# Self-attention scores in four PSUM banks, GpSimd's weighing behind VectorE's, and an early load of the second expert's W1

## The reference, cut to what matters

```
scores = where(causal, q @ k.T / sqrt(32), -1e30)
attn   = softmax(scores)
mask   = clip((256 + z - dist) / 256, 0, 1)      # z: one span per batch and head
attn   = attn * mask
attn   = attn / (attn.sum(-1) + 1e-8)
out    = attn @ v
```

## Time and profile before

| what | value |
|---|---|
| median of 3 runs | 3295.51 us (3294.92 to 3296.34) |
| the profiled execution | 3303.09 us |
| its span | 3301.3 us |
| TensorE busy, whole span | 2990.0 us (91%) |
| VectorE, ScalarE, GpSimd busy | 1859.6, 1063.0, 943.3 us |
| self-attention, about | 343 to 1830 us of the span |
| dispatch | 2577 to 2681 us |
| experts | 2681 to 3165 us |
| mean granted TensorE clock | 0.943 |

### The profile page before, as it was taken

The page is one execution under the profiler, slowest core; times in us unless marked ns, Lnnn a source line. Parts: engine busy times, 40 slices in busy tenths (PEclk is TensorE's granted clock), DMA queues, the critical chain, the costliest instruction groups (busy, mean ns, idle before and its releaser), DMA issues. The chain is left out here.

```text
span 3301.3 us, 54795 instructions
## 1 busy us (share of the span) xinstructions
PE 2990.0 (91%) x19242; PEld 1673.0 (51%) x19242; DVE 1859.6 (56%) x2220; ACT 1063.0 (32%) x2510; POOL 943.3 (29%) x606
## 2 busy tenths in 40 slices
PE   8998799999999999999999789999999787777778
PEld 6876333333333333333333678888888343333335
DVE  4355878787887878787883345555554510000038
ACT  3222344444444444444444223333333100101123
POOL 0000554445444444445454022222222000000013
PEclk9999899999999999999999889999999888878889
DMA  4453512121212212131200411111111669999954
GB/s 166 178 204 128 128 49 62 51 70 44 70 53 55 69 48 60 52 73 43 69 16 4 150 42 64 64 64 64 64 64 65 243 249 420 420 421 420 421 226 162
DMA packets 181219, 438.54 MB, mean 133 GB/s; under 512 B 17470, under 2 KB 51928, under 8 KB 156457
## 3 DMA queue, kind: packets, MB, share of 16 engines
q1 hardware_dynamic: 174057, 425.19, 36.8%
q10 hardware_dynamic: 6976, 10.75, 0.9%
HBM read 351.74 MB, written 83.89 MB: 132 GB/s over the span
## 5 line engine op out<-in xcount | busy, mean ns | idle before, releaser
L785 ACT ACTIVATE B_e<-B_pS 128x512 f32<-128x512 f32 (+3 forms) x1280 | 619.2, 534 | 850.0 <-PE B_pS L865 427.9
L640 POOL TENSOR_TENSOR B_em<-B_e,B_mask 128x1024 f32<-128x1024 f32 (+1 forms) x320 | 670.9, 2098 | 730.7 <-ACT B_e L785 693.9
L703 DVE TENSOR_REDUCE mx<-B_pM 128x4 f32<-128x2048 f32 (+2 forms) x299 | 588.9, 1969 | 38.7 <-PE B_pM L847 20.3
L865 PE MATMUL B_pS<-B_qs,B_ks 128*128 128x512 f32 (+3 forms) x1280 | 505.2, 447 | 43.4 <-issue 19.7
L696 DVE SCALAR_TENSOR_TENSOR B_em<-B_mask,B_e 128x1024 f32<-128x1024 f32 (+1 forms) x320 | 354.4, 1108 | 257.9 <-PE B_pN L895 256.3
L865 PEld LDWEIGHTS B_pS<-B_qs,B_ks 128*128 128x128 f32 x1280 | 227.8, 192 | 363.1 <-issue 238.5
L883 PE MATMUL B_pD<-B_e,B_tiny 128*32 128x512 f32 (+3 forms) x2560 | 310.0, 557 | 0.0
L889 PE MATMUL B_pD<-B_em,B_ones 128*32 128x512 f32 (+3 forms) x2560 | 301.2, 543 | 0.3 <-DVE B_em L696 0.3
L895 PE MATMUL B_pN<-B_em,B_v 128*32 128x512 f32 (+3 forms) x2560 | 293.4, 530 | 0.0
L2089 PE MATMUL E_pI<-ring,hT 128*32 128x512 f32 x1024 | 184.5, 815 | 101.1 <-DMA ring<-in_L_ffn_e_W_dram 57.8
L2012 DVE TENSOR_TENSOR E_ug<-E_pT,bT 128x32 f32 x32 | 5.7, 192 | 445.2 <-PE E_pT L2099 445.2
(11 more groups left out here) (288 smaller groups left out, 4764.2 us busy)
## 6 DMA issues: line engine op xcount, KB each, us to landing
ring<-in_L_ffn_e_W_dram SPq DMA_DIRECT2D x128, 1024.0 KB, 21.8
ring<-in_L_ffn_e_Wg_dram SPq DMA_DIRECT2D x64, 1024.0 KB, 23.6
B_qs<-q_hi SPq DMA_DIRECT2D x64, 256.0 KB, 4.5
B_ks<-k_hi SPq DMA_DIRECT2D x64, 256.0 KB, 3.9
E_xq<-xT_sc ACTq DMA_DIRECT2D x18, 512.0 KB, 10.3
ring<-x_sc SPq DMA_DIRECT2D x36, 256.0 KB, 2.6
qc<-in_x_dram SPq DMA_DIRECT2D x34, 256.0 KB, 2.7
qc<-a_sc SPq DMA_DIRECT2D x34, 256.0 KB, 3.0
```

What stands on the lines that cost most here:

```text
L640: nc.gpsimd.tensor_tensor(em[:, f % SLOTS_EM, DVE_HEADS:, w0:], e[:, f % SLOTS_E, DVE_HEADS:, w0:], mask[:, DVE_HEADS:, u0:u0 + BLK - w0], ...
L703: nc.vector.tensor_reduce(mx[:, :, qt, c], pM[:, :, 0:w], AX.X, ALU.max).then_inc(max_taken, 1)
L785: nc.scalar.activation(e[:, f % SLOTS_E, h, w0:], pS[:, h % SBANKS, w0:], ACT.Exp, scale=SCALE).then_inc(exp_ready, 1)
L865: last = nc.tensor.matmul(pS[:, h % SBANKS, w0:], ks[:, kb // NT, h, kb % NT * P:(kb % NT + 1) * P], qs[:, qb, h, w0:], start=True, stop=( ...
```

## The change

Self-attention:
- TensorE makes all four heads' scores of a step at once, into four banks: `B_pS` keeps two (heads 0 and 3), and heads 1 and 2 go to banks 2 and 3 of `B_pM`, which the units also use. So head 1's product waits until the last unit's maxima have been taken from banks 2 and 3 (`half_taken`), and a unit waits for the exponentials of heads 0 to 2 of its group's step (`exps_ahead`). The unit moves into the mix, between the products with 1e-8 and those with ones.
- VectorE reduces banks 2 and 3 first and then banks 0 and 1, two instructions for one. The reduction moves ahead of the weighing and of block 0's ramps; the other ramps stay at the end of the group, now right behind the weighing and the reciprocals. The reciprocals come in four parts over four groups.
- GpSimd's weighing of a step waits for VectorE's of the same step (`masked`).
- ScalarE's copies of the denominators and numerators after a block change places.

Experts:
- Six pieces of expert 0 are loaded at the start of dispatch and one behind each chunk's load. W1 of expert 1 goes to the upper half of `qc` during the end of dispatch (three pieces after the last chunk, the fourth after the output product) under a semaphore of its own; the ring's W1 pieces are then refilled with expert 2's while expert 1 runs. The first two experts are written out ahead of TensorE's loop.

```diff
-SBANKS = 2
+SBANKS = 4
+PARTS = 4
...
-        pS = ps("B_pS", [P, SBANKS, BLK], F32)
+        pS = ps("B_pS", [P, 2, BLK], F32)
+        score_bank = [pS[:, 0, :], pM[:, 2, :], pM[:, 3, :], pS[:, 1, :]]
...
-            events += [(min(ENDS[qb] + 5, STEPS + 1), "out", qb) for qb in range(BPB)]
+            events += [(min(ENDS[qb] + 3 + PARTS, STEPS + 1), "out", qb) for qb in range(BPB)]
...
                 pool.wait_ge(exp_ready, it * HPG * STEPS + HPG * (f + 1) + SBANKS)
                 pool.wait_ge(mixed, it * STEPS + STEPS + f + 1 - SLOTS_EM)
+                pool.wait_ge(masked, it * STEPS + f + 1)
                 nc.gpsimd.tensor_tensor(em[:, f % SLOTS_EM, DVE_HEADS:, w0:], e[:, f % SLOTS_E, DVE_HEADS:, w0:],
                                         mask[:, DVE_HEADS:, u0:u0 + BLK - w0], ALU.mult).then_inc(masked_last, 1)

             def divide(it, qb):
                 n = it * BPB + qb
-                pool.wait_ge(inverse, n * 2 + 2)
+                pool.wait_ge(inverse, (n + 1) * PARTS)
                 pool.wait_ge(num_out, n + 2)
                 pool.wait_ge(stored, 16 * n)
...
                         weigh(it, f)
-                    if f - 5 in ENDS:
-                        divide(it, block_end(f - 5))
+                    if f - 3 - PARTS in ENDS:
+                        divide(it, block_end(f - 3 - PARTS))
                 divide(it, BPB - 1)
...
                 w = BLK if c < qb else (qt + 1) * P
                 dve.wait_ge(max_ready, it * STEPS + n + 1)
-                nc.vector.tensor_reduce(mx[:, :, qt, c], pM[:, :, 0:w], AX.X, ALU.max).then_inc(max_taken, 1)
+                nc.vector.tensor_reduce(mx[:, 2:HPG, qt, c], pM[:, 2:HPG, 0:w], AX.X, ALU.max).then_inc(half_taken, 1)
+                nc.vector.tensor_reduce(mx[:, 0:2, qt, c], pM[:, 0:2, 0:w], AX.X, ALU.max).then_inc(max_taken, 1)
                 if n in ENDS:
+                    dve.wait_ge(half_taken, it * STEPS + n + 1)
                     dve.wait_ge(max_taken, it * STEPS + n + 1)
                     nc.vector.tensor_reduce(mm[:, :].rearrange("p (h q) -> p h q", h=HPG), mx[:, :, :, 0:qb + 1],
...
                 at_least(dve, mrow_loaded, 16 * r)
                 nc.vector.tensor_copy(mrow[:, :], pM[0:ROWS, 0, 0:P]).then_inc(mrow_ready, 1)
-            def invert(it, qb, half):
+            def invert(it, qb, part):
                 dve.wait_ge(den_out, it * BPB + qb + 2)
-                at = slice(half * BLK // 2, (half + 1) * BLK // 2)
+                at = slice(part * BLK // PARTS, (part + 1) * BLK // PARTS)
                 nc.vector.reciprocal(sums[:, 1, at], sums[:, 1, at]).then_inc(inverse, 1)
             RAMPS = 0
             dve.sem_inc(max_taken, EARLY)
+            dve.sem_inc(half_taken, EARLY)
             dve.sem_inc(neg_ready, EARLY_ROWS)
             take_turned(0)
             dve.wait_ge(spans_loaded, 16)
...
                         take_spans(it, (it + 1) * HPG, it + 2)
+                    n, later = unit_of(f)
+                    if n == 0 or (n - 1 in ENDS and not (final and later)):
+                        take_turned(rows_before(it + later, n))
+                    if not (final and later):
+                        reduce_unit(it + later, n)
                     if f == STEPS and not final:
                         dve.wait_ge(masked_last, it * STEPS + STEPS)
                         carry(dve, dve_carried)
                         ramp(it, 0, range(HPG), True)
-                    n, later = unit_of(f)
-                    if n == 0 or (n - 1 in ENDS and not (final and later)):
-                        take_turned(rows_before(it + later, n))
                     if not final or f < STEPS:
                         weigh(it, f)
-                    if f - 3 in ENDS:
-                        invert(it, block_end(f - 3), 0)
-                    if f - 4 in ENDS:
-                        invert(it, block_end(f - 4), 1)
-                    if final and later:
-                        continue
-                    reduce_unit(it + later, n)
-                    if f in plan:
+                    for part in range(PARTS):
+                        if f - 3 - part in ENDS:
+                            invert(it, block_end(f - 3 - part), part)
+                    if f in plan and not final:
                         c, h = plan[f]
                         if h == 0:
                             dve.wait_ge(masked_last, it * STEPS + ENDS[BPB - 2] + NT * (BPB - c) + 1)
                             carry(dve, dve_carried)
                         ramp(it, c, [h], h == HPG - 1)
-                invert(it, BPB - 1, 0)
-                invert(it, BPB - 1, 1)
+                for part in range(PARTS):
+                    invert(it, BPB - 1, part)

             with dve.Fori(0, ITS - 1) as it:
                 group(it, False)
...
-                    nc.scalar.activation(e[:, f % SLOTS_E, h, w0:], pS[:, h % SBANKS, w0:],
+                    nc.scalar.activation(e[:, f % SLOTS_E, h, w0:], score_bank[h][:, w0:],
...
                         exps(it, f, (0, 1))
-                    if f - 2 in ENDS:
-                        take(it, block_end(f - 2), 1)
+                    if f - 3 in ENDS:
+                        take(it, block_end(f - 3), 0)
                     n, later = unit_of(f - 1)
                     if n == 0 or (n - 1 in ENDS and not (final and later)):
                         row_out(rows_before(it + later, n), UNITS[n - 1][0])
                     if not final or f < STEPS:
                         exps(it, f, (2, 3))
                     if f - 2 in ENDS:
-                        take(it, block_end(f - 2), 0)
+                        take(it, block_end(f - 2), 1)
+                take(it, BPB - 1, 0)

             with act.Fori(0, ITS - 1) as it:
                 group(it, False)
...
-            def unit(it, n):
+            def unit(it, n, exps_ahead):
+
+                pe.wait_ge(exp_ready, exps_ahead)
...
-            def scores(it, f, heads):
+            def scores(it, f, units_made):
-                for h in heads:
+                for h in range(HPG):
...
-                    last = nc.tensor.matmul(pS[:, h % SBANKS, w0:], ks[:, kb // NT, h, kb % NT * P:(kb % NT + 1) * P],
+                    if h == 1:
+                        pe.wait_ge(half_taken, units_made)
+                    last = nc.tensor.matmul(score_bank[h][:, w0:], ks[:, kb // NT, h, kb % NT * P:(kb % NT + 1) * P],
-                        last = nc.tensor.matmul(pS[:, h % SBANKS, w0:w0 + P], identb[:, :], later_q[:, :],
+                        last = nc.tensor.matmul(score_bank[h][:, w0:w0 + P], identb[:, :], later_q[:, :],
-            def mix(it, f):
+            def mix(it, f, between):
...
                     cols = slice(h * DH, (h + 1) * DH)
                     nc.tensor.matmul(pD[cols, w0:], tiny[:, :], e[:, f % SLOTS_E, h, w0:],
                                      start=first, stop=False, tile_position=(0, h * DH))
+                between()
                 pe.wait_ge(masked, it * STEPS + f + 1)
                 pe.wait_ge(masked_last, it * STEPS + f + 1)
...
-            scores(0, 0, range(HPG))
-            scores(0, 1, range(HPG))
+            scores(0, 0, EARLY)
+            scores(0, 1, EARLY)
+                    n, later = unit_of(f)
-                        scores(it, f, (0, 1))
-                    mix(it, f - 2)
-                    n, later = unit_of(f)
+                        scores(it, f, (it + later) * STEPS + n if not (final and later) else (it + 1) * STEPS)
-                    if not final or f < STEPS:
-                        scores(it, f, (2, 3))
-                    if not (final and later):
-                        unit(it + later, n)
+                    exps_ahead = it * HPG * STEPS + HPG * f + 3 + SBANKS
+                    mix(it, f - 2, lambda: None if final and later else unit(it + later, n, exps_ahead))
...
+def load_second(eng, second, loaded, W1, pieces):
+
+    for k in pieces:
+        eng.dma_start(second[:, k, :], W1[1, k * P:(k + 1) * P, :]).then_inc(loaded, 16)
+
+
...
             sp.dma_start(wv[:, :, :], Wv.rearrange("(k p) n -> p k n", p=P)).then_inc(weights_loaded, 16)
             sp.dma_start(wo[:, :, :], Wo.rearrange("(k p) n -> p k n", p=P)).then_inc(weights_loaded, 16)
+            ahead = PIECES - (CHUNKS - 2)
+            load_expert(sp, ring, piece_loaded, 0, W1, Wg, W2, range(ahead))
             for n in range(2, CHUNKS):
                 sp.wait_ge(mixed, n - 1)
                 tokens(n)
-                load_expert(sp, ring, piece_loaded, 0, W1, Wg, W2, range(2 * (n - 2), 2 * (n - 1)))
+                load_expert(sp, ring, piece_loaded, 0, W1, Wg, W2, [ahead + n - 2])
+            sp.wait_ge(mixed, CHUNKS)
+            sp.wait_ge(total_ready, B)
+            load_second(sp, second, second_loaded, W1, range(KD - 1))
+            sp.wait_ge(made, nth["out"] + 1)
+            load_second(sp, second, second_loaded, W1, [KD - 1])
...
         def _(sp):
```

(53 more changed lines are left out.)

5 lines of the change are left out of this document (2 added, 3 removed).

## The result

The changed kernel takes 3359.47 us (median of 4 runs, 3357.67 to 3361.45), the one before beside it 3295.22: a ratio of 1.0195 [1.0182, 1.0207]. I forecast 3308 with 3248 to 3332 as the range. The direction was right and the size was not: about +64 us in place of +13.

What follows compares the result with a forecast made beforehand. TensorE, busy 1395 of 1478 us, bounds self-attention, full DMA engines the experts. Seven iterations +36, the last -11, dispatch and experts -12.8: +12.6 us, on the median of 3295.5 giving 3308, range 3248 to 3332.

Steps and rivals of the forecast that it cites:

- part 3: GpSimd's weighing, started behind VectorE's, blocks the minimum in six ramps of each self-attention iteration: +6.5 us an iteration.
- slower side: The changed kernel measures slower than the one before, beyond the 0.2% a measurement tells apart: chance 0.48.
- Groups 31 and 32: Self-attention before the unit of group 33: the blocked minimum makes VectorE late, 3.5 us of stall an iteration.
- Groups 35 and 36: Self-attention groups whose units are partly narrow: the blocked minimum costs 1.5 us an iteration.
- Iteration end: Groups 39 and 41: minimum and four reciprocals stand ahead of the next iteration's first reduction, 1.5 us an iteration.
- third rival: VectorE's ramps of heads 0 and 1 are blocked as well: 12 us in place of 6.5, 3347 us, chance 0.07.
- Part 1: Four score banks in self-attention: full step 4.63 us, a gain of 0.19 in 18 groups; together -1.3 us an iteration.
- part 4: Iteration's end: TensorE's 3.39 us wait for VectorE goes but returns at group 3; 0, gain up to 3.4.
- Part 2: Last self-attention iteration: ten full steps fall from 4.815 to 3.84 us, -10 us, and -1 for its first half.
- Part 5: Dispatch: four chunks' waits for tokens go, with one 1 MB piece ahead of each load, not two: -2.8 us.
- if not, 1 us is lost: Dispatch: the six early pieces should be through before the third chunk is wanted; otherwise 1 us is lost.
- Part 6: W1 loaded ahead at the end of dispatch: four pieces of 1.05 MB at 420 GB/s leave the experts' stream, -10.0 us.

Runs made afterwards that it cites:

- ramp_first: The changed kernel with VectorE's ramps of groups 29 to 41 moved between the reduction and the weighing, GpSimd's wait kept: 3283.97 us.
- experiments 5 and 6: The changed kernel with only the ramps that have a minimum ahead of VectorE's weighing (3292.25 us), or only those of heads 0 and 1 (3346.04 us).

## Why the prediction missed

**The mechanism of part 3 was right**, and so was the slower side. L684 came to 1.99 us, within the 1.5 to 2.5 I gave, in the wait put down to VectorE near groups 32 and 33. **The term was mis-sized**: 11.3 us an iteration (after against `ramp_first`, 78.9 in seven) in place of 6.5. By places:
- Groups 31 and 32: 5.6 (intervals 30 and 31 against `ramp_first`) for my 3.5. I had the waits; I had no clock in the sum. With it low for most of the way, from the late unit to the next mix took 4.98 us (1496.86 to 1501.84) and 3.58 at full clock (1433.07 to 1436.65): 1.4. The ramp's first half in group 31, 1.50 us behind the divide, was not in it either.
- Groups 35 and 36: 1.7 for 1.5.
- Iteration end: 3.3 for 1.5 (intervals 0, 1 and 39). Here too the clock was low behind the wait (0.50 from 1547.8 to 1552.0).
- Intervals 3 and 23, shorter than in `ramp_first`: 0.7 back. (The places are medians; the 11.3 is a mean.)
- The ramp of group 29: 1.5 for nothing. I had written that a first half is issued at once and gets ahead. It does, unless GpSimd's divide is running, as in group 31, or a reciprocal stands before it, as in group 29 after a block's end, by the change's own four parts. The timeline has it starting inside GpSimd's weighing:

```profile
1475.80 0.94 DVE L723 RECIPROCAL B_sums<-B_sums 128x128 f32<-128x128 f32 x1
1475.96 2.37 POOL L644 TENSOR_TENSOR B_em<-B_e,B_mask 128x1024 f32<-128x1024 f32 x1 [1.83 <-DVE B_em L700]
1476.66 1.95 DVE L677 TENSOR_SCALAR B_mask<-B_ndist,B_span 128x512 f32<-128x512 f32 x1
```

The reciprocal itself is hardly slowed by GpSimd's 2.37 us (0.94 for 0.89 where GpSimd is idle), nor are the reductions at 1.21; the ramp is. My third rival (12 in place of 6.5, 3347) came nearest by its number, but in the main for another reason: the ramps of heads 0 and 1 carry 0.3% to 0.6% of the 2.4 (experiments 5 and 6), and that is the ramp of group 29 above all.

**Part 1 was wrong in sign.** I had −1.3 us an iteration; `ramp_first` against before is +0.9, (1310.3 − 1304.3) / 7, with part 4 in it. Taken apart, the iteration's end (intervals 39, 0 and 1) gained 1.8 in the mean and the other 37 intervals lost 2.6, so this term was further off than the +0.9 shows. The full step did better than I worked out, 4.457 us (1406.10 to 1419.47 is three) for 4.63:

```profile
1406.10 1.07 PE L893 MATMUL B_pD<-B_e,B_tiny 128*32 128x512 f32 x8
...
1419.47 1.06 PE L893 MATMUL B_pD<-B_e,B_tiny 128*32 128x512 f32 x8
```

Most of what I missed is at the narrow steps. I costed them for the unit in a run, not for the turn behind it. In the old order the unit ended ahead of the next scores; now it waits for three full exponentials of the step ahead while the mix beside it is narrow, and the turn waits for that unit's two reductions. That is interval 22, 4.82 for 3.54, and interval 2 with 4.53 for 3.53; at group 24 of `ramp_first` the unit waits 0.40 us for ScalarE and the turn behind it 0.45 for the small maximum. No experiment took it apart by itself.

Together: by the traces self-attention took 75 us more, where my sum had 25. Of these 50 us, 34 are part 3 ((11.3 − 6.5) x 7), 15 are parts 1 and 4 ((0.9 + 1.3) x 7), and 1 is the last iteration.

**Part 2 was right**: the last iteration's full step is 3.85 us (1845.19 to 1876.01 is eight) for a forecast 3.84, and the iteration is 9.6 shorter for 11. Of what the banks gave, 4.8 went in the stall at its start, which part 3 carries over: in `ramp_first` it is 14.4 shorter.

```profile
1845.19 1.07 PE L893 MATMUL B_pD<-B_e,B_tiny 128*32 128x512 f32 x8
...
1876.01 1.07 PE L893 MATMUL B_pD<-B_e,B_tiny 128*32 128x512 f32 x8
```

**Part 4**: the wait of 3.39 for VectorE is gone, the second, for nothing that the profile shows, is still there with 3.23, and the wait came back at group 3 as forecast, with 2.78 us.

**Part 5** gave −2.9 for −2.8, by luck. The four waits I listed, 2.8 in sum, did go, but the third chunk now waits for its tokens behind the six early pieces; that was my "if not, 1 us is lost":

```profile
2683.80 14.00 PE L1857 MATMUL D_pU<-qc 128*128 128x512 f32 x32 [1.73 <-DMA qc<-xn_sc]
2698.01 27.30 PE L1857 MATMUL D_pU<-qc 128*128 128x512 f32 x63 [0.20 <-DMA qc<-xn_sc]
```

The waits fell by 0.9 only, and the other 2 us are products that ran at a higher clock in this execution (58.8 us busy for 60.9; granted clock 0.96 from the first chunk to the last for 0.93).

**Part 6 was right.** From the experts' first product to the next phase's output product took 489.9 us before and 480.0 after. Before:

```profile
2683.49 1.94 PE L2070 MATMUL E_pY<-E_zero,E_vT 128*32 128x512 f32 x8 [2.88 <-POOL E_vT L1997]
...
3173.43 2.79 PE L2313 MATMUL F_pO<-ring,F_o2T 128*32 128x512 f32 x12 [0.96 <-DMA ring<-in_L_ffn_c_bo_dram]
```

After:

```profile
2751.02 1.94 PE L2098 MATMUL E_pY<-E_zero,E_vT 128*32 128x512 f32 x8 [2.88 <-POOL E_vT L2025]
...
3231.00 2.79 PE L2354 MATMUL F_pO<-ring,F_o2T 128*32 128x512 f32 x12 [0.38 <-DVE F_o2T L2264]
```

Four pieces by 420 GB/s were 10.0, and 10.0 went.

## What to carry to other kernels

Look at what stands directly behind an instruction before you hang another engine's start on its end: GpSimd's wait for VectorE's weighing cost nothing with a reduction behind that weighing (3296). With the ramps behind it the kernel took 3359 us and with the ramps in front 3284; and the wait itself was worth 35 us in the first order (3359 against 3394) and over 100 in the second (3275 against 3381). When stalls of two or three microseconds are added to a full TensorE, look at its granted clock around them, and add what the products take more at the low level. And when an engine's order is rewritten, put the short instruction on which another engine waits, here the copy of the turned row, ahead of the long one that nobody wants yet: 0.27 us moved by one weighing gave 22 us.
